# Skip term added as an accumulated row, step bias inside the projection, one product moved to GpSimd, and the split of the MLP input in a row of its own

## Chip, cores and metric

The kernel runs on 1 core of one Trainium2 chip. The metric is device time in microseconds (us) of one execution. The engines are named as in the profile: PE is TensorE, DVE is VectorE, ACT is ScalarE, POOL is GpSimd, SP is SyncE (here it only issues DMAs).

## What is computed

Eight samples of 384 channels by 32x32 tokens (L = 1024). Layer 0 is a hybrid of a bidirectional selective scan and a depthwise convolution, layer 1 is causal attention and an MLP:

```python
def mamba(x, ...):                       # once forward, once on the flipped tokens
    u, z = split(x @ in_proj_w.T)
    u = silu(causal_conv4(u) + conv1d_b)
    dt, B, C = split(u @ x_proj_w.T, [24, 40])
    delta = softplus(dt @ dt_proj_w.T + dt_proj_b)
    h = exp(delta * A) * h + (delta * u) * B      # 16 states per channel, over 1024 tokens
    y = sum_n h * C + u * D_param                 # the skip term is u * D_param
    return (y * silu(z)) @ out_proj_w.T
x = x + res_scale * ((fwd + bwd) * scale_mod + sigmoid(dwconv3x3(xn) + dw_b) * xn)
t = t + attention(layernorm(t))          # 6 heads of 64, causal, 1024 tokens
t = t + gelu(layernorm(t) @ kron(c_fc_1, c_fc_2).T) @ kron(c_proj_1, c_proj_2).T
```

## The kernel before

Each engine has its own hand-written program; semaphores tie them. Channels lie on partitions as 3 tiles (k = 0, 1, 2) of 128, tokens along the free dimension, so most operations are 128x1024 in float32. One iteration b does layer 0 of sample b and, beside it, layer 1 of sample b-1; iteration 0 has no layer 1, iteration 8 no layer 0. An iteration has two stages.

**Preparation.** ACT copies the projected u (`copy_u`), DVE does the 3x3 taps (`depthwise`) and the 4-tap filters of both directions (`causal`), `silu_u` on ACT makes uc[0] and uc[1]. `step_size` on PE projects dt into PSUM (`dt_bank`); softplus of forward is max(x,0) + log(1 + exp(-|x|)): `soft_abs`, `soft_exp` and `soft_log` on ACT, `relu` (L977) and `soft_sum` (L983) on DVE. `in_project(b, 1)` on PE projects z in six groups (t = 6 to 11) of which ACT takes the SiLU (L917); groups 8 and 9 use PSUM banks that held `dt_bank[2]`. DVE then scales the gate (L1162), POOL adds it to the residual (L1237), DVE writes the skip term of both directions into y (`skip`, L1044 and L1047) and multiplies delta by u (`times_u`, L993).

**96 rows.** Row r is one state n of one direction d for one channel tile k. ACT makes the decay exp(delta * A) in PSUM (`decay`, L716), POOL multiplies du by the row of B (`input_row`, L1213) into one of five buffers hb, DVE scans (`scan_row`, L1055) and multiplies by the row of C (`output_row`, L1064), and POOL issues a DMA that adds the result to y (`sum_row`, L1224), LAG = 2 rows later. Decay r needs row r-2 finished on DVE; input r needs the DMA of row r-5 landed. Backward softplus sits in the first rows as items `step_bc`, `step_in`, `step_log`, `step_sum`. ACT also stores the backward relu over xres, for which the residual must first have been copied to DRAM.

Layer 1 of sample b-1 is a list of items, ITEMS, each with a weight. `slots()` spreads the list over the 96 rows in proportion to the running weight; each engine executes, in row r, its part of the items of SLOTS[r], some "early" (ahead of the row's own scan on DVE, or of decay r+1 on ACT), some after it. `scores n` and `values n` (n = 0 to 27) are the attention's groups; CROWDED are groups n for which `values n-1` and `scores n` share a row, where the scaling of the context comes late instead of early. PE has no work of its own in the rows and runs the items in list order.

Of the kernel before, what the change touches and what calls it, by code (L numbers as in the profile page):

```python
# [16 lines left out]
ALU = mybir.AluOpType  # L17
ACT = mybir.ActivationFunctionType
# [6 lines left out]
NS = 16  # L25
# [14 lines left out]
YIN = 16 * 2 * NS  # L40
# [10 lines left out]
for _h in range(0, NH, 2):  # L51
# [20 lines left out]
    + [("ln_mean", 1, 0.8), ("ln_var", 1, 0.9), ("ln_scale", 1, 0.9), ("mlp_in", 0, 1.395)]  # L72
# [20 lines left out]
STEP = ("step_bc", "step_in", "step_log", "step_sum")  # L93
# [9 lines left out]
def hybrid_block(nc, x, chan, scal, k128, k32, w_in, w_x, w_dt, w_out, wq, wk, wv, wo, fc1, fc2, pr1, pr2, kept, bc_rows, out):  # L103
    with ExitStack() as ctx:
# [20 lines left out]
        dt_w = [mixed[32:32 + RANK, 0:C], mixed[96:96 + RANK, 0:C]]  # L125
# [17 lines left out]
        dtr = [narrow[32:32 + RANK, :], narrow[96:96 + RANK, :]]  # L143
# [139 lines left out]
        def _(sp):  # L283
# [70 lines left out]
            def iteration(b, layer0, layer1, more):  # L354
                if layer0:
# [49 lines left out]
        def _(pe):  # L405
# [18 lines left out]
            def in_project(b, part):  # L424
# [27 lines left out]
            def step_size(b, d, k):  # L452
# [49 lines left out]
            def item(kind, n, b):  # L502
# [174 lines left out]
        def _(act):  # L677
# [62 lines left out]

            def copy_u(b):
# [28 lines left out]
            def item(kind, n, b, early):  # L770
# [3 lines left out]
                elif kind == "step_in" and not early:  # L774
# [4 lines left out]
                    act.activation(delta[1][:, n, :], dt_bank[KT + n][:, :], ACT.Relu,  # L779
                                   bias=vec[:, n, V_DTB:V_DTB + 1]).then_inc(relu_done, 1)  # L780
# [104 lines left out]
            def iteration(b, layer0, layer1, more):  # L885
                if layer0:
# [56 lines left out]
        def _(dve):  # L943
# [93 lines left out]
            def skip(b, d):  # L1037

                for k in range(KT):
                    dve.wait_ge(uc_ready, at(6, b, 3 * d + k + 1))  # L1040
                    dcol = vec[:, k, V_D:V_D + 1]
                    if d == 0:
                        dve.wait_ge(op_ready, at(6, b, 0))
                        dve.tensor_scalar(y[:, k, :], uc[0][:, k, :], dcol, None, ALU.mult).then_inc(yd_ready, 1)  # L1044
                    else:
                        dve.wait_ge(yd_ready, at(6, b, k + 1))
                        dve.scalar_tensor_tensor(out=y[:, k, :], in0=uc[1][:, k, :], scalar=dcol,  # L1047
                                                 in1=y[:, k, :], op0=ALU.mult, op1=ALU.add).then_inc(yd_ready, 1)

            def scan_row(b, r, n, k, d):  # L1050
# [4 lines left out]
                dve.tensor_tensor_scan(flow(d, buf), flow(d, buf), flow(d, hb[r % NHB][:, :]), 0.0,  # L1055
                                       ALU.mult, ALU.add).then_inc(scan_done, 1)

            def output_row(b, r, n, k, d):
# [5 lines left out]
                dve.tensor_tensor(hb[r % NHB][:, :], pBC[r % 2][:, :], c_row[g % 2][:, :], ALU.mult)\  # L1064
                   .then_inc(m2_done, 1)

            def item(kind, n, b, early):
                a = b - 1
                if kind == "step_sum" and not early:
                    soft_sum(b, 1, n)  # L1070
                    times_u(b, 1, n)
# [41 lines left out]
                elif kind == "mlp_in" and not early:  # L1113
# [30 lines left out]
            def iteration(b, layer0, layer1, more):  # L1144
                if layer0:
# [8 lines left out]
                    for k in range(KT):  # L1154
                        relu(b, k)
# [8 lines left out]
                    skip(b, 0)  # L1164
                    skip(b, 1)
# [149 lines left out]
```

## Time and profile before

| | |
|---|---|
| median of 3 runs | 4690.36 us (4688.07 to 4693.26) |
| profiled execution, time and span | 4690.52 us, span 4688.3 us |
| DVE busy | 4013.4 us, 86% of the span |
| PE / ACT / POOL busy | 69% / 52% / 61% |
| mean granted TensorE clock | 0.798 of full |
| one of the 6 middle iterations (first scan to first scan) | 549.6 us: 448.2 in its rows, 101.4 in preparation |
| rows of the first iteration | 349.5 us |
| after the last row of iteration 7 | 339.6 us |

The scan of row 0 starts at 144.0 us in iteration 0, at 610.35 in iteration 1, at 1158.65 in iteration 2, and every 549.6 us from there. Iteration 2 is used below for the preparation and the first rows, iteration 1 for the late rows. A row of the timeline is: start in us, duration in us, engine and line, operation, tiles, shapes, how many were merged, and in brackets how long the engine had been idle and which instruction ended that.

### The profile page before, as it was taken

Reading aid. Unit: us, or ns where it says so; the run is one execution under the profiler, and the core shown is the slowest. Engines: PE = TensorE matmul, PEld = TensorE weight load, DVE = VectorE, ACT = ScalarE, POOL = GpSimd, SP = SyncE. Lnnn points to the kernel's source line nnn. Section 1 sums busy time; section 2 is a strip of 40 time slices with the busy share of each in tenths; the row PEclk is TensorE's granted clock in tenths of the full one; section 3 lists DMA queues with packets and bytes.
Section 4 is the critical chain, followed back from the end, with each engine's and each line's share of the span. In section 5 each row is a group of like instructions: output and inputs, shape, how many; then the busy total and the mean of one; then the engine's idle time right before and its main releaser. Section 6 shows DMA issues by size and latency. Waiting matters only on the chain.

```text
span 4688.3 us, 38816 instructions
## 1 busy us (share of the span) xinstructions
PE 3251.8 (69%) x10858; PEld 1667.3 (36%) x10858; DVE 4013.4 (86%) x2961; ACT 2447.6 (52%) x3430; POOL 2847.9 (61%) x1671
## 2 busy tenths in 40 slices
PE   4100677767777768777677777877687776777797
PEld 1000235512354224532255223542245322552372
DVE  5999899989898999989999898988989899998221
ACT  3433446555464555655466544656556554665262
POOL 2798467764676647765577646766477655776100
PEclk8555778877888878878788778888788877888898
DMA  2799469982788639885599828886388855988100
GB/s 85 181 248 246 103 144 206 216 210 77 186 197 216 163 101 207 201 216 131 133 207 207 211 80 188 199 217 167 98 200 200 216 147 123 206 201 186 51 6 14
DMA packets 223126, 772.34 MB, mean 165 GB/s; under 512 B 24666, under 2 KB 40330, under 8 KB 222890
## 3 DMA queue, kind: packets, MB, share of 16 engines
q0 software_dynamic: 110592, 402.70, 44.2%
q1 hardware_dynamic: 112298, 366.90, 24.4%
q8 instruction: 98, 1.61, 0.1%
q14 instruction: 138, 1.13, 0.1%
HBM read 339.60 MB, written 27.26 MB: 78 GB/s over the span
## 4 chain that ended last, share of the span: by engine, by line
DVE 33%; PE 23%; issue 22%; POOL 8%; ACT 8%; DMA 5%; DVEq 1%; SPq 0%; ACTq 0%; POOLq 0%
DVE pBC L1055 16%; POOL hb L1213 7%; PE pW L482 5%; DMA y<-hb 5%; PE pW L421 4%; PE pW L449 4%; DVE stat L1095 3%; PE pW L561 2%; DVE hb L1064 2%; DVE du_f L1008 2%; ACT pBC L716 1%; PE pW L586 1%; ACT area L865 1%; ACT L867 1%; DVE du_f L1162 1%
## 5 line engine op out<-in xcount | busy, mean ns | idle before, releaser
L1055 DVE TENSOR_TENSOR_SCAN pBC<-pBC,hb 128x1024 f32<-128x1024 f32 x768 | 1756.6, 2287 | 90.0 <-ACT pBC L716 53.9
L1224 POOL DMA_DIRECT2D y<-hb x768 | 722.8, 941 | 912.9 <-DVE hb L1064 844.6
L1213 POOL TENSOR_TENSOR hb<-du_f,b_row 128x1024 f32<-128x1024 f32 x384 | 1039.8, 2720 | 61.2 <-DVE du_f L993 48.6
L1213 POOL TENSOR_TENSOR hb<-uc_b,b_row 128x1024 f32<-128x1024 f32 x384 | 1000.1, 2605 | 48.6 <-DMA y<-hb 34.4
L1064 DVE TENSOR_TENSOR hb<-pBC,c_row 128x1024 f32<-128x1024 f32 x768 | 940.6, 1225 | 46.7 <-DVE pBC L1055 3.2
L716 ACT ACTIVATE pBC<-xres,vec 128x1024 f32<-128x1024 f32 x384 | 427.1, 1117 | 337.2 <-DVE hb L1064 336.3
L561 PE MATMUL pW<-area,pt 128*128 128x64 f32 x3456 | 446.4, 284 | 157.9 <-ACT pt L831 157.9
L716 ACT ACTIVATE pBC<-delta,vec 128x1024 f32<-128x1024 f32 x384 | 427.5, 1116 | 198.8 <-DVE hb L1064 198.7
L449 PE MATMUL pW<-area,consts 128*128 128x512 f32 x288 | 162.3, 723 | 487.0 <-ACT area L876 356.3
L561 PEld LDWEIGHTS pW<-area,pt 128*128 128x128 f32 x3456 | 417.5, 198 | 215.6 <-ACT pt L831 207.3
L1095 DVE TENSOR_REDUCE stat<-pW 128x1 f32<-128x640 f32 (+7 forms) x361 | 257.5, 750 | 166.5 <-PE pW L485 166.4
L482 PE MATMUL pW<-area,w_ko 128*128 128x512 f32 (+3 forms) x540 | 308.1, 708 | 123.8 <-ACT prob L841 85.0
L841 ACT ACTIVATE prob<-pW,stat 128x640 f32<-128x640 f32 (+7 forms) x361 | 265.3, 742 | 244.1 <-DVE stat L1095 244.1
L1232 POOL TENSOR_TENSOR du_f<-du_f,hb 128x1024 f32<-128x1024 f32 x64 | 193.4, 3022 | 254.0 <-ACT hb L730 248.5
L441 PE MATMUL pW<-area,xn_area 128*128 128x512 f32 x576 | 290.9, 665 | 62.5 <-DVE area L1138 55.4
L482 PE MATMUL pW<-area,v_w 128*128 128x512 f32 (+3 forms) x542 | 254.7, 600 | 45.3 <-ACT prob L841 45.0
L449 PEld LDWEIGHTS pW<-area,consts 128*128 128x128 f32 x288 | 64.4, 235 | 584.9 <-issue 462.4
L831 ACT COPY pt<-pW 128x512 f32<-128x512 f32 x378 | 209.1, 590 | 117.9 <-PE pW L498 113.9
L498 PE MATMUL pW<-consts,prob 128*128 128x128 f32 x1512 | 245.7, 311 | 29.3 <-ACT xn_area L757 16.5
L498 PEld LDWEIGHTS pW<-consts,prob 128*128 128x128 f32 x1512 | 199.0, 164 | 122.4 <-issue 119.3
L1008 DVE SCALAR_TENSOR_TENSOR du_f<-area,vec,du_f 128x1024 f32<-128x1024 f32 x128 | 227.6, 1846 | 0.0
L757 ACT ACTIVATE xn_area<-pW,stat 128x64 f32<-128x64 f32 x384 | 102.2, 310 | 220.4 <-DVE stat L1106 177.3
(158 smaller groups left out, 4969.1 us busy)
## 6 DMA issues: line engine op xcount, KB each, us to landing
y<-hb POOLq DMA_DIRECT2D x768, 512.0 KB, 7.0
b_row<-bc_rows SPq DMA_DIRECT2D x256, 512.0 KB, 5.8
c_row<-bc_rows SPq DMA_DIRECT2D x256, 512.0 KB, 5.0
area<-in_x SPq DMA_DIRECT2D x8, 1536.0 KB, 15.2
xres<-in_x SPq DMA_DIRECT2D x8, 1536.0 KB, 6.3
kept_residual<-xres SPq DMA_DIRECT2D x8, 1536.0 KB, 5.6
xres<-kept_residual SPq DMA_DIRECT2D x8, 1536.0 KB, 11.9
out_x<-xa SPq DMA_DIRECT2D x8, 1536.0 KB, 7.1
```

Source lines behind the costliest of these rows:

```text
L441: mm = pe.matmul(pW[:, t % 4, :], ip_w[:, k, 128 * m:128 * m + 128], xnp[:, k, 1 + 16 * c:17 + 16 * c, 1:1 + WW], start=(k == 0), stop=(k ...
L449: mm = pe.matmul(bank, ones_c, src[:, k, toks], start=(k == 0), stop=(k == KT - 1))
L482: pe.matmul(bank[:, lo:hi], q, kT[:, h // 2, lo - c0:hi - c0], start=True, stop=hi != end)
L498: mm = pe.transpose(prob_bank(b, half)[:, 128 * j:128 * j + 128], prob[:, half * HALF + 128 * j:half * HALF + 128 * j + 128], ident)
L561: mm = pe.matmul(pW[:, 3, DH * t:DH * t + DH], pt[:, c0 + 128 * j:c0 + 128 * j + 128], vtok[:, j, DH * h:DH * h + DH], start=(j == 0), sto ...
L716: act.activation(pBC[r % 2][:, :], delta[d][:, k, :], ACT.Exp, scale=vec[:, k, V_A + n:V_A + n + 1]).then_inc(da_ready, 1)
L1008: dve.scalar_tensor_tensor(out=acc, in0=win, scalar=w, in1=acc, op0=ALU.mult, op1=ALU.add).then_inc(dw_step, 1)
L1055: dve.tensor_tensor_scan(flow(d, buf), flow(d, buf), flow(d, hb[r % NHB][:, :]), 0.0, ALU.mult, ALU.add).then_inc(scan_done, 1)
L1064: dve.tensor_tensor(hb[r % NHB][:, :], pBC[r % 2][:, :], c_row[g % 2][:, :], ALU.mult)\
L1095: mx = dve.tensor_reduce(stat[:, 0, st:st + 1], scores_bank(b, n)[:, c0:c0 + 128 * (i + 1)], AX, ALU.max, negate=True)
L1213: pool.tensor_tensor(hb[r % NHB][:, :], du[d][:, k, :], b_row[g % 2][:, :], ALU.mult)\
L1224: pool.dma_start(y[:, k, :], hb[r % NHB][:, :], accum_op=ALU.add).then_inc(y_in[k], 16)
```

## The change

- `skip` leaves DVE. ACT computes u * D_param: forward into y ahead of decay 0, backward into hb[0..2] between decay 0 and the items of row 0. POOL adds the backward part to y with three more DMAs (`sum_skip`), issued ahead of the input of row 2. Rows use the buffers from hb[3] on (`slot`), so input r waits from row 2 on, at first for these DMAs.
- `relu` leaves DVE. The bias enters the projection as a 25th row, and `soft_sum` of the forward direction does max(x, 0) + log part in one operation, out of PSUM. With it, z groups 8 and 9 on PE wait for the third such sum.
- `times_u` of the backward direction is done by POOL, in rows 6, 9 and 12 (`step_du`).
- The DVE part of `mlp_in` becomes an item `mlp_split` of weight 0.7 behind it. The weights' sum grows from 103.16 to 103.86, by which items move by up to one row from row 17 on.

```diff
+for _k in range(KT):
+    SLOTS[6 + 3 * _k].append(("step_du", _k))
@@ ITEMS
-    + [("ln_mean", 1, 0.8), ("ln_var", 1, 0.9), ("ln_scale", 1, 0.9), ("mlp_in", 0, 1.395)]
+    + [("ln_mean", 1, 0.8), ("ln_var", 1, 0.9), ("ln_scale", 1, 0.9), ("mlp_in", 0, 1.395), ("mlp_split", 0, 0.7)]
@@ PE, in_project
                     elif t >= 8:
-                        pe.wait_ge(relu_done, at(6, b, 3))
-                        pe.wait_ge(sp_abs, at(6, b, 3))
+                        pe.wait_ge(delta_ready, at(6, b, 3))
@@ ACT
+            def skip(b, d):
+                for k in range(KT):
+                    act.wait_ge(uc_ready, at(6, b, 3 * d + k + 1))
+                    act.wait_ge(op_ready if d == 0 else delta_ready, at(6, b, 0 if d == 0 else k + 1))
+                    act.activation(y[:, k, :] if d == 0 else hb[k][:, :], uc[d][:, k, :], ACT.Identity,
+                                   scale=vec[:, k, V_D:V_D + 1]).then_inc(yd_ready, 1)
...
                     silu_u(b, 1)
                     act.preload_act_table_set(LOG_EXP)
+                    skip(b, 0)
                     decay(b, 0)
+                    skip(b, 1)
@@ DVE, soft_sum
                 if d == 0:
+                    dve.scalar_tensor_tensor(out=delta[0][:, k, :], in0=dt_bank[k][:, :], scalar=0.0,
+                                             in1=soft[0][k][:, :], op0=ALU.max, op1=ALU.add).then_inc(delta_ready, 1)
@@ DVE, iteration
-                    for k in range(KT):
-                        relu(b, k)
                     causal(b, 12, 24)
...
-                    skip(b, 0)
-                    skip(b, 1)
                     for k in range(KT):
-                        times_u(b, 0, k)
+                        times_u(b, k)
@@ POOL
+                elif kind == "step_du":
+                    pool.wait_ge(delta_ready, at(6, b, 4 + n))
+                    pool.wait_ge(yd_ready, at(6, b, 6))
+                    pool.tensor_tensor(du[1][:, n, :], delta[1][:, n, :], uc[1][:, n, :], ALU.mult).then_inc(du_ready, 1)
...
-                if r >= NHB:
-                    pool.wait_ge(y_in[(r - NHB) % KT], at(YIN, b, 16 * ((r - NHB) // KT + 1)))
+                if r >= NHB - KT:
+                    pool.wait_ge(y_in[(r + KT - NHB) % KT], at(YIN, b, 16 * ((r + KT - NHB) // KT + 1)))
...
+                        if r == NHB - KT:
+                            for skip_k in range(KT):
+                                sum_skip(b, skip_k)
```

On PE, the z groups 8 and 9 stand in the preparation of an iteration (the loop's body; area is the normalised input, xn_area the weights). Before:

```order
67 L441 MATMUL pW<-area,xn_area 128x512 [waits xd_evac]
68 L441 MATMUL pW<-area,xn_area 128x512 x2
69 L441 MATMUL pW<-area,xn_area 128x512 [waits sp_abs,relu_done]
70 L441 MATMUL pW<-area,xn_area 128x512 x2
71 L441 MATMUL pW<-area,xn_area 128x512 [waits sp_abs,relu_done]
72 L441 MATMUL pW<-area,xn_area 128x512 x2
```

and after the change:

```order
67 L447 MATMUL pW<-area,xn_area 128x512 [waits xd_evac]
68 L447 MATMUL pW<-area,xn_area 128x512 x2
69 L447 MATMUL pW<-area,xn_area 128x512 [waits delta_ready]
70 L447 MATMUL pW<-area,xn_area 128x512 x2
71 L447 MATMUL pW<-area,xn_area 128x512 [waits delta_ready]
72 L447 MATMUL pW<-area,xn_area 128x512 x2
```

Nothing moved on PE, but what groups 8 and 9 wait for did: DVE's relu stood ahead of its backward filters, the sum stands behind them.

On ACT, from the backward SiLU (L738, L746 after the change) to the first backward softplus item, before:

```order
123 L738 ACTIVATE uc_b<-uc_b,vec 128x1024 [waits cv_step]
124 L920 ACT_TABLE_LOAD
125 L713 ISA
126 L716 ACTIVATE pBC<-delta,vec 128x1024 [waits delta_ready,m2_done]
127 L688 REGISTER_ALU
128 L689 COPY narrow<-pW 24x1024 [waits xd_ready]
129 L690 COPY pt<-pW 32x1024
130 L716 ACTIVATE pBC<-delta,vec 128x1024 [waits delta_ready,m2_done]
```

and after the change:

```order
125 L746 ACTIVATE uc_b<-uc_b,vec 128x1024 [waits cv_step]
126 L935 ACT_TABLE_LOAD
127 L754 ACTIVATE y<-area,vec 128x1024 [waits op_ready,uc_ready] x3
128 L721 ISA
129 L724 ACTIVATE pBC<-delta,vec 128x1024 [waits delta_ready,m2_done]
130 L752 REGISTER_ALU
131 L754 ACTIVATE hb<-uc_b,vec 128x1024 [waits delta_ready,uc_ready]
132 L752 REGISTER_ALU
133 L754 ACTIVATE hb<-uc_b,vec 128x1024 [waits delta_ready,uc_ready]
134 L752 REGISTER_ALU
135 L754 ACTIVATE hb<-uc_b,vec 128x1024 [waits delta_ready,uc_ready]
```

Three operations stand ahead of decay 0 (pBC), three more between it and the copies that feed the backward step size.

On DVE, late in the rows (a scan is printed here as SCALAR_TENSOR_TENSOR pBC<-pBC,hb), from the last layer-norm scaling to the split of the MLP input, before:

```order
714 L1064 TENSOR_TENSOR hb<-pBC,c_row 128x1024 [waits scan_done,c_in1]
715 L1086 TENSOR_TENSOR area<-area,pW 128x3x512 [waits ln_rs] x2
716 L1114 ISA
717 L1115 TENSOR_TENSOR prob<-pW,pt 128x1024 [waits xr_step]
718 L1116 REGISTER_ALU
719 L1117 CAST pt<-prob 128x1024 [waits xr_step]
```

and after the change:

```order
698 L1084 TENSOR_TENSOR area<-area,pW 128x3x512 [waits ln_rs] x2
699 L1051 REGISTER_ALU
700 L1054 SCALAR_TENSOR_TENSOR pBC<-pBC,hb 128x1024 [waits m1_done,da_ready]
701 L1063 TENSOR_TENSOR hb<-pBC,c_row 128x1024 [waits scan_done,c_in1]
702 L1051 REGISTER_ALU
703 L1054 SCALAR_TENSOR_TENSOR pBC<-pBC,hb 128x1024 [waits m1_done,da_ready]
704 L1063 TENSOR_TENSOR hb<-pBC,c_row 128x1024 [waits scan_done]
705 L1112 ISA
706 L1113 TENSOR_TENSOR prob<-pW,pt 128x1024 [waits xr_step]
```

Two whole rows (scan and product) now stand between the scaling and the split. A little ahead of this, `ln_mean 1` moved from a row of its own (73) into row 72, right behind the last `wo` item; `wo 0` moved from row 69 to 68.

## Rows read from the trace of the kernel before

**Rows 1.** The page, part 1: busy time, share of the span, instructions.

```profile
PE 3251.8 (69%) x10858; PEld 1667.3 (36%) x10858; DVE 4013.4 (86%) x2961; ACT 2447.6 (52%) x3430; POOL 2847.9 (61%) x1671
```

**Rows 2.** Timeline of DVE, iteration 2, preparation and first rows.

```profile
1117.69 2.46 DVE L977 TENSOR_SCALAR delta<-pBC,vec 128x1024 f32<-128x1024 f32 x2
...
1121.27 2.06 DVE L1031 TENSOR_SCALAR uc_b<-area,vec 128x1024 f32<-128x1024 f32 x3
...
1134.02 3.48 DVE L983 TENSOR_TENSOR delta<-delta,hb 128x1024 f32<-128x1024 f32 x3
...
1143.10 6.24 DVE L1044 TENSOR_SCALAR y<-area,vec 128x1024 f32<-128x1024 f32 x3
...
1152.85 3.48 DVE L993 TENSOR_TENSOR du_f<-delta,area 128x1024 f32<-128x1024 f32 x3
1158.65 2.30 DVE L1055 TENSOR_TENSOR_SCAN pBC<-pBC,hb 128x1024 f32<-128x1024 f32 x1 [2.31 <-POOL hb L1213]
...
1162.20 2.29 DVE L1055 TENSOR_TENSOR_SCAN pBC<-pBC,hb 128x1024 f32<-128x1024 f32 x1
...
1187.76 2.29 DVE L1055 TENSOR_TENSOR_SCAN pBC<-pBC,hb 128x1024 f32<-128x1024 f32 x1
```

**Rows 3.** Timeline of ACT, the same stretch.

```profile
1132.54 3.21 ACT L738 ACTIVATE uc_b<-uc_b,vec 128x1024 f32<-128x1024 f32 x3
1135.77 1.28 ACT L920 ACT_TABLE_LOAD   x1
...
1143.92 1.00 ACT L690 COPY pt<-pW 32x1024 f32<-32x1024 f32 x1
...
1147.70 1.11 ACT L699 ACTIVATE area<-pW,vec 128x1024 f32<-128x1024 f32 x1 [1.77 <-PE pW L462]
...
1166.45 2.94 ACT L708 ACTIVATE area<-area 128x1024 f32<-128x1024 f32 x3
```

**Rows 4.** Timeline of PE, z projection (two passes a matmul).

```profile
1112.80 8.39 PE L441 MATMUL pW<-area,xn_area 128*128 128x512 f32 x12
1121.40 10.61 PE L441 MATMUL pW<-area,xn_area 128*128 128x512 f32 x24 [0.21 <-DVE delta L977]
```

**Rows 5.** Busy time by stretch: engines, then PEclk, DMA share, GB/s.

```profile
1112.90:1121.30 8.40, 8.29 (x12) 3.18 (x12) 8.40 (x8) 8.36 (x9) 0.20 (x1) 0.65 0.40 148
```

**Rows 6.** Timeline of POOL, iteration 2: gate sum, first inputs, a row's DMA.

```profile
1138.78 9.36 POOL L1237 TENSOR_TENSOR xres<-xres,du_f 128x1024 f32<-128x1024 f32 x3 [25.68 <-DVE du_f L1162]
...
1154.21 8.94 POOL L1213 TENSOR_TENSOR hb<-du_f,b_row 128x1024 f32<-128x1024 f32 x3 [6.08 <-DVE du_f L993]
...
1191.61 0.88 POOL L1224 DMA_DIRECT2D y<-hb  x1 [10.58 <-DVE hb L1064]
```

**Rows 7.** DVE groups by line and shape: count, busy us, mean ns, idle before.

```profile
L993 DVE TENSOR_TENSOR uc_b<-xres,uc_b 128x1024 f32<-128x1024 f32 x24 | 63.6, 2652 | 0.8
```

**Rows 8.** Line L1055, all scans: shortest, median, longest ns, first and last start.

```profile
L1055 DVE TENSOR_TENSOR_SCAN pBC<-pBC,hb x768: 2275/2289/2299, 144.0 to 4345.2; 128x1024 f32<-128x1024 f32 x192
```

**Rows 9.** The page, part 6, DMAs: count, size, us to landing.

```profile
y<-hb POOLq DMA_DIRECT2D x768, 512.0 KB, 7.0
```

**Rows 10.** Timeline of DVE, iteration 1, second layer norm and MLP input.

```profile
945.27 1.76 DVE L1078 TENSOR_TENSOR area<-xa,pW 128x1536 f32<-128x1536 f32 x1 [1.17 <-PE pW L449]
...
969.05 1.23 DVE L1115 TENSOR_TENSOR prob<-pW,pt 128x1024 f32<-128x1024 f32 x1 [9.13 <-ACT pt L857]
```

**Rows 11.** Timeline of DVE, iteration 1, attention: first and last of six waits.

```profile
739.92 1.29 DVE L1095 TENSOR_REDUCE stat<-pW 128x1 f32<-128x512 f32 x2 [0.19 <-PE pW L485]
...
894.16 1.29 DVE L1095 TENSOR_REDUCE stat<-pW 128x1 f32<-128x256 f32 x2 [1.67 <-PE pW L485]
```

**Rows 12.** Timelines of DVE and ACT, iteration 0; the last row is scan 4.

```profile
103.03 2.48 DVE L977 TENSOR_SCALAR delta<-pBC,vec 128x1024 f32<-128x1024 f32 x2 [8.33 <-ACT hb L699]
...
107.73 2.95 ACT L708 ACTIVATE hb<-hb 128x1024 f32<-128x1024 f32 x3
...
169.93 2.29 DVE L1055 TENSOR_TENSOR_SCAN pBC<-pBC,hb 128x1024 f32<-128x1024 f32 x1
```

More of the change, by code:

```diff
@@ L39 @@
 NHB = 5
-YIN = 16 * 2 * NS
+YIN = 16 * (2 * NS + 1)
 LAG = 2
@@ L124, in hybrid_block @@
         mixed = sb("mixed", [128, C])
[L125 removed]
+        dt_w = [mixed[32:33 + RANK, 0:C], mixed[96:97 + RANK, 0:C]]
         kout_w = mixed[64:64 + KI, 0:C]
@@ L142, in hybrid_block @@
         narrow = sb("narrow", [128, L])
-        dtr = [narrow[32:32 + RANK, :], narrow[96:96 + RANK, :]]
+        dtr = [narrow[32:33 + RANK, :], narrow[96:97 + RANK, :]]
         rr = narrow[64:64 + KI, :]
@@ L273, in rows, with slot @@
             return [(r, r // DROWS, r % DROWS // KT, r % KT) for r in range(ROWS)]
+        def slot(r):
+            return (r + KT) % NHB
         def flow(d, ap):
@@ L368, in iteration @@
                         sp.wait_ge(du_ready, at(6, b, 3))
+                        sp.wait_ge(yd_ready, at(6, b, 3))
                         load_next(b + 1)
@@ L458, in step_size @@
                 if g >= 4:
-                    pe.wait_ge(relu_done, at(6, b, g - 1))
-                    pe.wait_ge(sp_abs, at(6, b, g - 1))
+                    if g == 4:
+                        pe.wait_ge(delta_ready, at(6, b, 3))
+                    else:
+                        pe.wait_ge(relu_done, at(3, b, 1))
+                        pe.wait_ge(sp_abs, at(6, b, 4))
                 for c in range(2):
@@ L698, in soft_abs @@
                 act.wait_ge(dt_ready, at(6, b, 3 * d + k + 1))
-                act.activation(soft[d][k][:, :], dt_bank[KT * d + k][:, :], ACT.Abs,
-                               bias=vec[:, k, V_DTB:V_DTB + 1]).then_inc(sp_abs, 1)
+                act.activation(soft[d][k][:, :], dt_bank[KT * d + k][:, :], ACT.Abs).then_inc(sp_abs, 1)
             def soft_exp(b, d, k):
@@ L778, in item @@
                     act.wait_ge(kept_out, at(16, b, 16))
-                    act.activation(delta[1][:, n, :], dt_bank[KT + n][:, :], ACT.Relu,
-                                   bias=vec[:, n, V_DTB:V_DTB + 1]).then_inc(relu_done, 1)
+                    act.activation(delta[1][:, n, :], dt_bank[KT + n][:, :], ACT.Relu).then_inc(relu_done, 1)
                 elif kind == "step_log" and not early:
@@ L1035, in causal @@
                                                  op0=ALU.mult, op1=ALU.add).then_inc(cv_step, 1)
-            def skip(b, d):
-                for k in range(KT):
[L1040 to L1048, printed above, removed]
             def scan_row(b, r, n, k, d):
@@ L1112, in item @@
                                              in1=xa[:, m, toks], op0=ALU.add, op1=ALU.add).then_inc(wo_add, 1)
-                elif kind == "mlp_in" and not early:
+                elif kind == "mlp_split" and not early:
                     dve.wait_ge(xr_step, at(5, a, 1))
@@ L1153, in iteration @@
                     depthwise(b, 8, 18)
-                    for k in range(KT):
-                        relu(b, k)
                     causal(b, 12, 24)
@@ L1219, in sum_row, with sum_skip @@
                 pool.wait_ge(m2_done, at(ROWS, b, r + 1))
-                if r < KT:
-                    pool.wait_ge(yd_ready, at(6, b, 6))
-                else:
-                    pool.wait_ge(y_in[k], at(YIN, b, 16 * (r // KT)))
-                pool.dma_start(y[:, k, :], hb[r % NHB][:, :], accum_op=ALU.add).then_inc(y_in[k], 16)
+                pool.wait_ge(y_in[k], at(YIN, b, 16 * (r // KT + 1)))
+                pool.dma_start(y[:, k, :], hb[slot(r)][:, :], accum_op=ALU.add).then_inc(y_in[k], 16)
+            def sum_skip(b, k):
+                pool.wait_ge(yd_ready, at(6, b, 4 + k))
+                pool.dma_start(y[:, k, :], hb[k][:, :], accum_op=ALU.add).then_inc(y_in[k], 16)
             def iteration(b, layer0, layer1, more):
@@ L1297 @@
         "w_x": np.concatenate([xp[RANK:], xp[:RANK]], 0).T,
-        "w_dt": i0["dt_proj_w"].T,
+        "w_dt": np.concatenate([i0["dt_proj_w"].T, i0["dt_proj_b"][None]], 0),
         "w_out": i0["out_proj_w"].T,
```

38 lines of the change are left out of this document (16 added, 22 removed).

## Prediction

> **What bounds it now.** I read the page first, then the timeline of DVE, then the same stretches of ACT, PE and POOL. The page [rows 1] shows DVE busy 86% of the span and everybody else at 69% or less. The timeline of DVE shows why: a row of scan and product takes 3.5 us of DVE (scan 1 starts 3.55 after scan 0), 96 rows follow each other almost without idle time, and in the preparation (depthwise, filters, sums, gate, skip, product with u) DVE waits for nobody but POOL, 2.3 us ahead of scan 0 [rows 2]. So a microsecond taken from DVE is a microsecond of the kernel, as long as no other engine's work has to be done by then. That condition is the whole question here, because the change puts work on ACT and makes PE wait.
>
> **What leaves DVE, per iteration.** relu: from 1117.69 to 1121.27, 3.6 us. skip: from 1143.10 to 1152.85, 9.75 us. [rows 2] The backward product with u: 3 x 2.65 = 7.95 us [rows 7]. Together 21.3 us, over eight iterations 170 us. If all of it counted, the kernel would be at 4520.
>
> **The preparation, on the clock of iteration 2.** DVE ends the depthwise taps at 1117.7 as before. The filters last 12.75 us (1121.27 to 1134.02) and now start 3.6 earlier: 1130.4. The three new sums read PSUM and SBUF; no such row exists, the nearest are the old relu (3.6 for three) and the old sums (3.48), so 3.5: 1133.9. [rows 2]
>
> PE: z groups 8 to 11 were 10.61 us from 1121.4 [rows 4]. They now wait for the third sum, 1133.9, so 12.5 us later. PE has then been idle for some 13 us. How it restarts is in the trace: the first z groups took 8.39 us for 12 passes, with a granted clock of 0.65, where 5.3 would be the time at the full level [rows 4, 5]. So a restart costs between nothing and 3.1 us; I take 2.3, as the longer idle time speaks for most of it. PE ends at 1146.9.
>
> ACT can't pass these groups: its order is fixed. Last SiLU of z 1147.5, three backward SiLUs 3.2, table 1.3: 1152.0. Three skip products: no row has them, but three 128x1024 activations in a row took 3.2: 1155.2. Decay 0, 1.1 as each of those: 1156.3. Three more skip products: 1159.5. Two copies, 2.0: 1161.5. Decay 1: 1162.6. The first backward |x| comes 2.8 after the copies (1144.9 to 1147.7): 1164.3. Two triples (abs, exp, relu; 3.1 each): 1170.5. Decay 2: 1171.6. Third triple: 1174.7. Three logs, 2.9: 1177.6. Decay 3: 1178.7. [rows 3]
>
> POOL and DVE by themselves would be earlier. The gate sum on POOL moves with DVE's gate, 3.5 earlier, and ends at 1144.6 instead of 1148.1 [rows 6]; the product with u can start there (it was at 1152.85), and scan 0 came 5.8 after its start [rows 2]: 1150.4. The decay is ready at 1156.3, so **ACT sets scan 0**, only 2.3 us ahead of the old 1158.65. Then scan 1 waits for decay 1 (1162.6), scan 2 for decay 2 (1171.6), scan 3 for decay 3 (1178.7). From there DVE: row 3.5, two sums 2.5 (1.2 each as the forward ones), layer-norm mean 3.3 (two of 1.76, overlapping a little) [rows 10], scan 4 at 1188.0. Before it was at 1187.76 [rows 2]. **So the 21 us that leave DVE give nothing: +0.2 us per iteration**; DVE stands idle instead, in rows 0 to 3, for the decays.
>
> What this hides: the skip's DMAs. They are issued from about 1158 on and land 7.0 later [rows 9], so input 2 is done by 1168, ahead of decay 2 at 1171.6. If the ACT chain were 6 us shorter, it would cost. The three products on POOL in rows 6, 9 and 12 are 2.65 each; POOL runs two rows ahead, and waits 10.58 us for DVE at the first [rows 6]. At the other two its lead of about one row (3.5) takes the 2.65. I cost them at nothing; with the cover gone, up to 8 us per iteration.
>
> A page of the Trainium skill speaks against this step. Perfetto Trace Analysis, section Optimizing Scalar/DVE Operations, warns that DVE and GpSimd share an SBUF read port and that moving operations between those two "might not help". By that rule, the page's own words, the 8 us would only change place. What the trace shows is that the DVE product took 2.65 us beside POOL's work instead of the 1.16 of the forward one, but the scans keep 2275 to 2299 ns throughout [rows 2, 7, 8]: in the rows DVE isn't blocked by POOL. The sum goes by this.
>
> **Iteration 0** differs: there DVE waited 8.33 us at the relu for ACT [rows 12]. Now the filters fill that wait and the third sum follows the logs, which end at 110.7: 112.0. With the same chain as above (44.7 us from third sum to decay 3, 54.1 to scan 4) scan 4 is at 166.1; it was at 169.9 [rows 12]. Gain 3.8 us.
>
> **The late rows** (iterations 1 to 7). DVE waited 9.13 us for the MLP input to come out of PE and ACT [rows 10]. Two rows now stand there, 7.0 us: that much is gained. Against it, the second layer-norm mean stands right behind the last wo item. Its averages start only then, and the row that covered them but for 1.17 us [rows 10] is gone: 3.5 us lost. wo 0, a row earlier, waits a little more: 0.3. Net 3.2 gained at the split. Behind it ACT's Gelu and table loads share the pacing with DVE, and one row less stands ahead of the first Gelu; I take 0.9 as given back. 2.3 per iteration; bounds 0 and 3.5.
>
> **Attention.** Of its pairs of groups in adjacent rows, those whose scores come late make DVE wait, between 0.19 and 1.67 us, six times in iteration 1 [rows 11]. The new slots have eight such pairs, as before, but other groups: five instead of six begin with a two-block group. At unchanged odds that is -0.5 us per iteration. Each wait is either near 0.2 or near 1.7, so the bounds are wide: from -6 to +6.3.
>
> **Sum.** Iteration 0: -3.8. Seven iterations: +0.2 - 2.3 - 0.5 = -2.6 each, -18.2. The tail, 339.6 us, keeps its order and its time. From the profiled execution's 4690.5: 4668.5; the median of the runs shown is 0.2 us below that execution, so **4668**.
>
> **Rivals.**
> - *The chain through the z groups is longer.* If the four z groups run at the low level throughout, they take 21.2 us instead of 12.9: +8.3 on ACT's chain and on every scan 4, eight times, 66 us: 4734. Point of decision: 2.8 us more per iteration than I have and the change is slower than before. For it: in rows 0 to 3 nothing covers ACT any more. Against: the trace's restart was over after 8.4 us. 12%.
> - *The chain does not bind*, DVE and POOL set the start: scan 0 at 1150.4 and rows 2 and 3 shorter by 7.95, 16.4 per iteration and 2.8 in seven, 151 us: 4540. It needs ACT 16 us faster than the rows give. 5%.
> - *Attention waits fall badly* (+6.3 in each of seven, 4715), 8%, *or well* (-6, 4630), 10%.
> - *The gain at the split is given back* to ACT's Gelu chain: 2.3 x 7 = 16, 4684. For it: rows behind the split wait for decays already. 12%.
> - *The product on POOL blocks DVE or falls into a full POOL*: 8 per iteration, 64 us, 4732. This is the skill's warning above turned into a time. 3%.
>
> **How the numbers follow.** My forecast has 50%, its own range 4645 to 4690. Cases outside 4622 to 4715 hold 12 + 5 + 3 = 20%, hence the range. 0.2% is about what a measurement of this kernel can tell from no change: 4681 to 4700. Faster: most of the 50 (42), attention well 10, chain not binding 5, part of the split case 4, so 61%. Same: 7 of the 50, 8 of the split case and a little of attention, 16%. Slower: 23%.
>
> **What the profile after would show.** z groups of L447 starting near 1134 less the shift of the earlier iterations; DVE idle before the first four scans, released by ACT's decays, 15 to 20 us in all; scan 4 as far from the end of the last row as before; the wait at the split about 2 us instead of 9.13, the wait at the second mean about 4.6 instead of 1.17; POOL's new products with no scan waiting behind them. I am wrong if scans 0 to 3 wait for POOL or the DMA instead, if z ends more than 15 us after the third sum, or if DVE's row times change.

## The result: 4751 us, 1.3% slower than before

| | before | changed |
|---|---|---|
| median (lowest to highest, 4 runs each) | 4691.4 us (4688.1 to 4693.3) | 4751.4 us (4746.4 to 4753.5) |
| ratio to before, 95% interval | | 1.0128 (1.0116 to 1.0140) |
| span of the profiled execution | 4688.3 us | 4748.2 us |

The page of the changed kernel, part 1, against [rows 1]:

```profile
PE 3277.8 (69%) x10858; PEld 1671.2 (35%) x10858; DVE 3901.6 (82%) x2865; ACT 2492.2 (52%) x3478; POOL 2935.0 (62%) x1719
```

DVE is 112 us less busy and the kernel 60 us longer: its idle time grew by 172 us. The starts of the scans say where the 60 are. I cut the trace at scans 0, 4, 66, 77 and 95 and added up iterations 1 to 7. The first column runs from the end of the last product of one iteration to scan 0 of the next:

| us | last product to scan 0 | 0 to 4 | 4 to 66 | 66 to 77 | 77 to 95 | iteration 0 | all |
|---|---|---|---|---|---|---|---|
| my sum | -16 | +17.5 | -3.5 | -22.4 | +6.3 | -3.8 | -22 |
| measured | -21.7 | +53.8 | -5.1 | +5.2 | +16.7 | +11.5 | +60 |

Three places miss: rows 0 to 4 (+36 against the sum), the late rows (+38) and iteration 0 (+15).

First the preparation and rows 0 to 4 of iteration 2, in the timelines of the changed kernel; DVE, to [rows 2]:

```profile
1151.34 2.34 DVE L994 SCALAR_TENSOR_TENSOR delta<-pBC,hb 128x1024 f32<-128x1024 f32 x2
1153.60 1.21 DVE L994 SCALAR_TENSOR_TENSOR delta<-pW,hb 128x1024 f32<-128x1024 f32 x1
...
1165.13 5.66 DVE L1005 TENSOR_TENSOR du_f<-delta,area 128x1024 f32<-128x1024 f32 x3 [4.64 <-POOL xres L1238]
1176.28 2.30 DVE L1054 TENSOR_TENSOR_SCAN pBC<-pBC,hb 128x1024 f32<-128x1024 f32 x1 [5.50 <-ACT pBC L724]
...
1182.49 2.30 DVE L1054 TENSOR_TENSOR_SCAN pBC<-pBC,hb 128x1024 f32<-128x1024 f32 x1 [2.58 <-ACT pBC L724]
...
1192.59 2.30 DVE L1054 TENSOR_TENSOR_SCAN pBC<-pBC,hb 128x1024 f32<-128x1024 f32 x1 [6.54 <-ACT pBC L724]
...
1199.38 2.30 DVE L1054 TENSOR_TENSOR_SCAN pBC<-pBC,hb 128x1024 f32<-128x1024 f32 x1 [1.68 <-ACT pBC L724]
...
1202.92 7.01 DVE L998 TENSOR_TENSOR xres<-xres,area 128x1024 f32<-128x1024 f32 x2
1209.85 3.40 DVE L1076 TENSOR_TENSOR xn_area<-xa,pW 128x1536 f32<-128x1536 f32 x2
1213.18 2.28 DVE L1054 TENSOR_TENSOR_SCAN pBC<-pBC,hb 128x1024 f32<-128x1024 f32 x1
```

PE, to [rows 4], and ACT, to [rows 3]:

```profile
1154.87 12.10 PE L447 MATMUL pW<-area,xn_area 128*128 128x512 f32 x24 [13.88 <-DVE delta L994]
```

```profile
1167.00 0.60 ACT L932 ACTIVATE zs<-pW 128x512 f32<-128x512 f32 x1 [1.99 <-PE pW L447]
1167.49 3.22 ACT L746 ACTIVATE uc_b<-uc_b,vec 128x1024 f32<-128x1024 f32 x3
1170.72 1.28 ACT L935 ACT_TABLE_LOAD   x1
1172.02 3.23 ACT L754 ACTIVATE y<-area,vec 128x1024 f32<-128x1024 f32 x3
1175.15 1.10 ACT L724 ACTIVATE pBC<-delta,vec 128x1024 f32<-128x1024 f32 x1
1176.19 3.21 ACT L754 ACTIVATE hb<-uc_b,vec 128x1024 f32<-128x1024 f32 x3
...
1198.24 2.15 ACT L724 ACTIVATE pBC<-delta,vec 128x1024 f32<-128x1024 f32 x2
```

ACT's chain is the one I built: z starts when the third sum (L994) ends and takes 12.1 us, then come SiLU, table load, skip products and decay 0. Each of scans 0 to 3 waits for a decay, 16.3 us in all. What doesn't fit stands behind scan 3: the last two backward sums (L998) take 7.01 us, not 2.5. POOL, to [rows 6], runs the new product (L1201) and an input (L1212) beside them:

```profile
1203.91 2.64 POOL L1201 TENSOR_TENSOR uc_b<-xres,uc_b 128x1024 f32<-128x1024 f32 x1
1206.30 2.54 POOL L1212 TENSOR_TENSOR hb<-du_f,b_row 128x1024 f32<-128x1024 f32 x1
```

Over the whole kernel, the groups of the changed kernel (first) and of before (second; those of [rows 7] have left DVE): count, busy us, mean ns:

```profile
L998 DVE TENSOR_TENSOR xres<-xres,area 128x1024 f32<-128x1024 f32 x24 | 65.9, 2771 | 2.6 <-ACT area L716 2.6
```

```profile
L983 DVE TENSOR_TENSOR xres<-xres,area 128x1024 f32<-128x1024 f32 x24 | 31.9, 1329 | 0.0
```

In iteration 0 POOL's four tap sums started beside DVE's ten tap steps (two SBUF inputs each) in the kernel before too, but DVE's backward filters came later, behind its wait at the relu. Now the filters follow the tap steps almost at once. DVE, POOL and ACT before (first), then POOL, ACT and DVE of the changed kernel:

```profile
82.66 12.04 DVE L1008 SCALAR_TENSOR_TENSOR du_f<-area,vec,du_f 128x1024 f32<-128x1024 f32 x10
...
85.04 19.32 POOL L1232 TENSOR_TENSOR du_f<-du_f,hb 128x1024 f32<-128x1024 f32 x4 [10.56 <-ACT hb L730]
...
96.92 1.15 ACT L730 ACTIVATE hb<-area,vec 128x1024 f32<-128x1024 f32 x1 [3.53 <-POOL du_f L1232]
```

```profile
83.85 32.07 POOL L1233 TENSOR_TENSOR du_f<-du_f,hb 128x1024 f32<-128x1024 f32 x4 [10.56 <-ACT hb L738]
...
108.49 1.15 ACT L738 ACTIVATE hb<-area,vec 128x1024 f32<-128x1024 f32 x1 [16.61 <-POOL du_f L1233]
...
81.48 12.03 DVE L1020 SCALAR_TENSOR_TENSOR du_f<-area,vec,du_f 128x1024 f32<-128x1024 f32 x10
...
95.42 10.84 DVE L1046 SCALAR_TENSOR_TENSOR uc_b<-area,vec,uc_b 128x1024 f32<-128x1024 f32 x9
120.10 2.36 DVE L994 SCALAR_TENSOR_TENSOR delta<-pBC,hb 128x1024 f32<-128x1024 f32 x2 [13.84 <-ACT hb L716]
```

DVE's filters keep their 1.2 us each, and POOL's sums take 32.1 us instead of 19.3. The whole difference lies in the first of the four, which takes 24.6 us instead of 11.9; the other three take 2.3 to 2.4 each in both kernels. The first ends 2.2 us after DVE's last step of this kind, before (94.7 and 96.9) and after (106.3 and 108.5). ACT waits 16.6 us for the tap, and the sum 13.8 us for ACT. In e1 below, where the forward sums stand ahead of the filters again, POOL's four are back at 19.3.

Late rows. Before, iteration 1, beside [rows 10]: DVE's only wait at the wo items, and PE at the averages:

```profile
926.79 0.75 DVE L1111 SCALAR_TENSOR_TENSOR xa<-pW,vec,xa 128x512 f32<-128x512 f32 x1 [1.03 <-PE pW L421]
...
940.69 7.12 PE L449 MATMUL pW<-xa,consts 128*128 128x512 f32 x12 [3.64 <-DVE xa L1111]
```

Changed, iteration 2: DVE at the first wo item, PE at the averages, DVE at the second mean (two operations) and the split:

```profile
1499.05 0.75 DVE L1109 SCALAR_TENSOR_TENSOR xa<-pW,vec,xa 128x512 f32<-128x512 f32 x1 [3.58 <-PE pW L428]
...
1517.13 8.38 PE L455 MATMUL pW<-xa,consts 128*128 128x512 f32 x12 [5.07 <-DVE xa L1109]
...
1522.66 1.75 DVE L1076 TENSOR_TENSOR area<-xa,pW 128x1536 f32<-128x1536 f32 x1 [5.58 <-PE pW L455]
1525.55 1.75 DVE L1076 TENSOR_TENSOR area<-xa,pW 128x1536 f32<-128x1536 f32 x1 [1.14 <-PE pW L455]
...
1547.08 1.22 DVE L1113 TENSOR_TENSOR prob<-pW,pt 128x1024 f32<-128x1024 f32 x1 [2.52 <-ACT pt L872]
```

The split waits 2.5 us instead of 9.1, near the 2 that I wrote. The mean waits 6.7, where I wrote 4.6, and wo 0 3.6.

### The profile page after: what moved, and what is told of

It is laid out like the page before. It is cut to its first block, busy times and chain, and to the rows that moved or that the text cites. A ratio compares the mean times of both kernels' runs of the same rounds, so it can differ in the third digit from the quotient of the medians.

```text
span 4748.2 us, 38811 instructions
## 1 busy us (share of the span) xinstructions
PE 3277.8 (69%) x10858; PEld 1671.2 (35%) x10858; DVE 3901.6 (82%) x2865; ACT 2492.2 (52%) x3478; POOL 2935.0 (62%) x1719
## 4 chain that ended last, share of the span: by engine, by line
DVE 28%; PE 27%; issue 20%; ACT 11%; POOL 8%; DMA 5%; DVEq 1%; SPq 0%; ACTq 0%; POOLq 0%
DVE pBC L1054 13%; PE pW L491 6%; POOL hb L1212 6%; DMA y<-hb 5%; PE pW L455 4%; DVE stat L1093 3%; PE pW L447 3%; PE pW L570 3%; PE pW L428 2%; ACT pBC L724 2%; DVE du_f L1020 1%; DVE hb L1063 1%; PE pW L595 1%; ACT area L880 1%; PE pW L471 1%
## 5 line engine op out<-in xcount | busy, mean ns | idle before, releaser
L1220 POOL DMA_DIRECT2D y<-hb x768 | 738.1, 961 | 934.3 <-DVE hb L1063 885.1
L1212 POOL TENSOR_TENSOR hb<-du_f,b_row 128x1024 f32<-128x1024 f32 x384 | 1044.8, 2735 | 42.7 <-DMA y<-hb 30.1
L1212 POOL TENSOR_TENSOR hb<-uc_b,b_row 128x1024 f32<-128x1024 f32 x384 | 1009.0, 2628 | 22.0 <-DMA y<-hb 21.9
L1063 DVE TENSOR_TENSOR hb<-pBC,c_row 128x1024 f32<-128x1024 f32 x768 | 940.2, 1224 | 44.7 <-DVE pBC L1054 0.5
L447 PE MATMUL pW<-area,xn_area 128*128 128x512 f32 x576 | 303.1, 689 | 168.0 <-DVE delta L994 113.1
L1233 POOL TENSOR_TENSOR du_f<-du_f,hb 128x1024 f32<-128x1024 f32 x64 | 206.5, 3226 | 249.6 <-ACT hb L738 244.1
L491 PE MATMUL pW<-area,w_ko 128*128 128x512 f32 (+3 forms) x540 | 281.6, 656 | 106.7 <-ACT prob L856 70.5
L491 PE MATMUL pW<-area,v_w 128*128 128x512 f32 (+3 forms) x542 | 264.9, 619 | 74.3 <-ACT prob L856 74.3
L447 PEld LDWEIGHTS pW<-area,xn_area 128*128 128x128 f32 x576 | 125.3, 223 | 351.2 <-issue 213.0
```

The source lines that it names most:

```text
L447: mm = pe.matmul(pW[:, t % 4, :], ip_w[:, k, 128 * m:128 * m + 128], xnp[:, k, 1 + 16 * c:17 + 16 * c, 1:1 + WW], start=(k == 0), stop=(k ...
L491: pe.matmul(bank[:, lo:hi], q, kT[:, h // 2, lo - c0:hi - c0], start=True, stop=hi != end)
L1063: dve.tensor_tensor(hb[slot(r)][:, :], pBC[r % 2][:, :], c_row[g % 2][:, :], ALU.mult)\
L1212: pool.tensor_tensor(hb[slot(r)][:, :], du[d][:, k, :], b_row[g % 2][:, :], ALU.mult)\
L1220: pool.dma_start(y[:, k, :], hb[slot(r)][:, :], accum_op=ALU.add).then_inc(y_in[k], 16)
```

## Experiments

Two theories about the 60 us stood first. **A, the z wait**: z groups 8 and 9 wait for a sum that stands behind the filters, and ACT, in fixed order, carries that to all decays. **B, DVE and POOL**: the work put on POOL is what costs. A third, **C**: the split's row costs more than it gives. The table has medians in us and ratios to before with their intervals; the stage columns are iteration 2 in one profiled execution ("gap" is the first column of the table above, the others go from scan to scan).

| | median | ratio | gap to scan 0 | 0 to 4 | 66 to 77 | 77 to 95 |
|---|---|---|---|---|---|---|
| before | 4691 | 1 | 101.4 | 29.1 | 65.5 | 77.6 |
| changed | 4751 | 1.0128 | 98.1 | 36.9 | 66.5 | 80.0 |
| sum_first | 4668 | 0.9953 (0.9936 to 0.9970) | 92.9 | 30.6 | 66.4 | 80.2 |
| du_a_row_later | 4745 | 1.0115 (1.0098 to 1.0132) | 98.1 | 34.6 | 66.5 | 80.3 |
| split_with_mlp_in | 4728 | 1.0079 (1.0063 to 1.0096) | 99.3 | 35.7 | 65.5 | 77.6 |
| before_with_split | 4713 | 1.0046 (1.0030 to 1.0063) | 101.3 | 29.1 | 66.4 | 80.2 |
| sum_first_old_rows | 4641 | 0.9888 (0.9870 to 0.9906) | 92.9 | 30.6 | 65.2 | 79.2 |
| before_z_wait | 4751 | 1.0125 (1.0107 to 1.0143) | 103.6 | 34.7 | 65.0 | 79.1 |
| changed_skip_on_dve | 4722 | 1.0063 (1.0045 to 1.0081) | 99.9 | 31.9 | 66.5 | 80.2 |
| sum_first_product_on_dve | 4670 | 0.9956 (0.9940 to 0.9971) | 92.9 | 32.0 | 66.5 | 80.3 |
| sums_from_psum | 4615 | 0.9831 (0.9813 to 0.9848) | 92.9 | 23.2 | 66.4 | 80.2 |
| best_product_row_later | 4617 | 0.9838 (0.9825 to 0.9852) | 92.9 | 28.3 | 65.0 | 79.1 |
| before_skip_on_act | 4667 | 0.9950 (0.9934 to 0.9965) | 96.1 | 32.0 | 65.0 | 79.1 |

**e1_sum_first.** The changed kernel, forward sums ahead of the backward filters:

```diff
                     depthwise(b, 8, 18)
-                    causal(b, 12, 24)
                     for k in range(KT):
                         soft_sum(b, 0, k)
+                    causal(b, 12, 24)
```

> The changed kernel, but the three forward sums (L994) stand on DVE ahead of the twelve backward filter steps instead of behind them. Theory A (the start of the rows is set by ACT's chain, which hangs on the z groups, which wait for the third sum): the sums wait about 2 us for ACT's logs, then z groups 8 to 11 start some 12 us earlier; ACT gets to decay 0 ahead of DVE and POOL, and from one of the iterations 1 to 7 about 5 to 9 us go: 4751 - 8 x 7 = about 4695 (4680 to 4710). Rival B (the wait of the z groups is harmless, the rows are held by work moved to GpSimd and by its DMAs): within 8 us of the changed kernel, 4743 to 4760.

83 us less than the changed kernel, more than A expected: 38 ahead of scan 0 and 44 in rows 0 to 4 of iterations 1 to 7, 9 in iteration 0, while other rows give back 7. No scan of rows 0 to 3 waits for a decay any more. The timeline of DVE shows what it waits for instead:

```profile
1143.08 5.64 DVE L1005 TENSOR_TENSOR du_f<-delta,area 128x1024 f32<-128x1024 f32 x3 [6.97 <-POOL xres L1238]
...
1158.08 2.30 DVE L1054 TENSOR_TENSOR_SCAN pBC<-pBC,hb 128x1024 f32<-128x1024 f32 x1 [2.36 <-POOL hb L1212]
...
1161.55 3.96 DVE L998 TENSOR_TENSOR xres<-xres,area 128x1024 f32<-128x1024 f32 x1
...
1168.97 7.01 DVE L998 TENSOR_TENSOR xres<-xres,area 128x1024 f32<-128x1024 f32 x2
```

POOL, the input of row 2:

```profile
1155.64 2.34 POOL L1212 TENSOR_TENSOR hb<-du_f,b_row 128x1024 f32<-128x1024 f32 x1 [2.12 <-DMA y<-hb]
```

The product with u waits for POOL's gate sum, scan 2 for POOL's input, and the input for the skip's DMA. The backward sums are as long as in the changed kernel or longer.

**e6_before_z_wait.** The kernel before, with nothing changed but what z groups 8 and 9 wait for:

```diff
                     elif t >= 8:
-                        pe.wait_ge(relu_done, at(6, b, 3))
-                        pe.wait_ge(sp_abs, at(6, b, 3))
+                        pe.wait_ge(delta_ready, at(6, b, 3))
```

> The kernel before with one edit: z groups 8 and 9 wait for the third forward sum, as in the change, instead of for the relu. Nothing is added to ACT and nothing leaves DVE. Theory A (z late by 16 us drags ACT's chain past DVE by itself): decay 2 some 8 us behind DVE's need, scan 3 and scan 4 about 8 us later in each of eight iterations: 4691 + 60 = 4750 (4730 to 4760). Rival B (ACT had the room, only z late together with six skip products on ACT costs): under 4700.

That wait alone costs 60 us, so A holds. 16 lie ahead of scan 0 and 38.5 in rows 0 to 4 of iterations 1 to 7, and 10 in iteration 0; other rows give back 3. PE and ACT in iteration 2 (the third sum of DVE ended at 1156.2):

```profile
1156.23 12.22 PE L440 MATMUL pW<-area,xn_area 128*128 128x512 f32 x24 [17.26 <-DVE delta L982]
1172.24 7.05 PE L642 MATMUL pW<-uc_b,xp_w 128*56 128x512 f32 x12 [3.80 <-ACT uc_b L737]
```

```profile
1168.98 3.21 ACT L737 ACTIVATE uc_b<-uc_b,vec 128x1024 f32<-128x1024 f32 x3
...
1179.33 1.00 ACT L688 COPY narrow<-pW 24x1024 f32<-24x1024 f32 x1 [4.71 <-PE pW L642]
```

A late z makes the backward SiLU late, its projection on PE later, and the copies and decays behind it.

**e3_split_with_mlp_in and e4_before_with_split.** The split's item shares a row with `mlp_in` again (weights 0.0 and 1.395, the old sum), and the kernel before gets the split's row and nothing else:

```diff
-    ... ("mlp_in", 0, 1.395), ("mlp_split", 0, 0.7)]
+    ... ("mlp_in", 0, 0.0), ("mlp_split", 0, 1.395)]
```

> The changed kernel, but the split shares the row and the weight of mlp_in again, so that all items but the products with u stand in their old rows. Theory A (the moved items cost: in rows 66 to 95 the changed kernel is 3.4 us per iteration slower than the kernel before): 7 x 3.4 less, 4728. Rival B (my forecast, the split's own row gains 2.3 us per iteration and the loss comes from what ACT and the clock do elsewhere): 16 us more, 4767.

> The kernel before with only the new item mlp_split of weight 0.7, which moves the slots as in the change. Theory A (the moved items cost 3 to 4 us in each of seven iterations by themselves): 4691 + 24 = 4715. Rival B (my forecast for this part alone, late rows -2.3 and attention -0.5 per iteration): 4671. If it is within 5 us of 4691, the late rows' loss in the changed kernel comes from its other parts.

The two agree: the split's row, with the shift of the items that it brings, costs 22 to 23 us, 3 per iteration. C holds, beside A.

**e5_sum_first_old_rows.** e1 and e3 together.

> Both repairs together: the forward sums ahead of the backward filters and the split in the row and weight of mlp_in, all else as in the changed kernel. If the two losses are separate, the gains add: 4668.5 - 23 = 4645 (4638 to 4652), 1% faster than the kernel before. If they overlap (the late rows are slower only because of what happened earlier in an iteration), between 4655 and 4668.

The two gains add up, and 5 us more come on top (27.6 instead of 23).

**e7_changed_skip_on_dve and e12_before_skip_on_act.** The skip moved by itself: in the changed kernel back to DVE (no skip DMAs), and in the kernel before to ACT, with its DMAs. Of e7 this is the part on ACT; DVE's skip and POOL's old buffer order come back with it:

```diff
                     act.preload_act_table_set(LOG_EXP)
-                    skip(b, 0)
                     decay(b, 0)
-                    skip(b, 1)
...
```

> The changed kernel with the skip term back on DVE and without its DMAs and the shifted buffers. Theory A (in rows 0 to 3 ACT's chain sets the pace, 6.4 us of it are the skip products; DVE has the room for the skip while it waits): 8 x 5 to 8 x 6.4 less than 4751, 4700 to 4711, though DVE does 9.8 us more work per iteration. Rival B (DVE's work sets the pace): 8 x 6 to 8 x 9.8 more, 4799 or above.

> The kernel before with the skip term alone moved: ACT computes it, GpSimd adds the backward part with three more DMAs, buffers shifted; relu, bias, products, z waits and items as before. Theory A (ACT had room for six more activations as long as z came early; DVE then waits only for the gate sum of GpSimd): scan 0 some 4.7 us earlier, 8 x 4.6 = 37 us less, 4654 (4645 to 4665). Rival B (the skip's DMAs or ACT hold rows 1 to 3, so the part costs by itself): 4691 or more.

The sign turns with what binds. Where z waits, 9.8 us more on DVE in each iteration make the kernel 29 us faster, since ACT's chain gets 6.4 us shorter. I expected 40 to 51: rows 0 to 4 give 34 in iterations 1 to 7, but DVE's skip now stands ahead of scan 0, and the gap takes 11 back. Where z doesn't wait, the move to ACT gains 24 us. That is less than the 37 I expected: the gap shrinks by 5.3, but scan 2 now waits 2.4 us for an input that waits for the skip's DMA, and in all 0 to 4 is 2.9 longer.

**e2_du_a_row_later.** POOL's products in rows 7, 10 and 13, a row behind the sums' rows.

```diff
 for _k in range(KT):
-    SLOTS[6 + 3 * _k].append(("step_du", _k))
+    SLOTS[7 + 3 * _k].append(("step_du", _k))
```

> The changed kernel, but the three backward products with u on GpSimd stand in rows 7, 10 and 13 instead of 6, 9 and 12. GpSimd runs ahead, so the product of row 6 runs while DVE does the second and third backward sum, which took 7.0 us for two. Theory A (an operation of DVE with two SBUF inputs and a GpSimd operation exclude each other): only the input of row 6 stands beside the sums then, the pair takes 4.7 us or less, 2.3 us less per iteration, 18 us: 4733. Rival B (the 7.0 us come from waiting for ACT or from the DMAs): no change, 4751. Rival C (GpSimd has no room in rows 7 to 13): slower than 4751.

Rows 0 to 4 get 2.3 us shorter, as expected; the kernel gets 6 us faster, not 18. Iteration 0 came out 3 longer, and rows 4 to 66 gave back 9 in iterations 1 to 7. In iteration 2 these are waits of DVE: before scans 6.1 us for 4.7, before the attention's reductions 10.5 for 8.8. Why they grow I have not found.

**e8_sum_first_product_on_dve and e9_sums_from_psum.** Both start from e1. e8 has the three products back on DVE, behind each sum. e9 leaves the products on POOL and lets the backward sum read PSUM instead of xres, so that one input lies in SBUF and not two; it reads half a projection twice and so leaves out a part of the backward step size. It waits for all three relus and the last projection. Its edit, shortened and without the waits:

```diff
-                    dve.tensor_tensor(delta[1][:, k, :], delta[1][:, k, :], soft[1][k][:, :], ALU.add)
+                    dve.scalar_tensor_tensor(out=delta[1][:, k, :]...,
+                                             in0=pW[:, 3:4, :].broadcast_to([128, 2, HALF]), scalar=0.0,
+                                             in1=soft[1][k][:, :]..., op0=ALU.max, op1=ALU.add)
```

> The kernel of e1_sum_first, but the three backward products with u are back on DVE, each right behind its sum, and none is on GpSimd. Theory A (the move to GpSimd gave almost nothing, because GpSimd's product holds up the sum beside it: sums and products took 12.2 us of DVE before, the sums alone 11.0 in e1_sum_first): 1.2 us more per iteration, 10 us, 4678 (4670 to 4685). Rival B (the move is worth what left DVE, 7.95 us per iteration): 4732.

> The kernel of e1_sum_first, but the three backward sums take max(x,0) from one PSUM bank (read twice) instead of from xres, so they have one SBUF input instead of two. It leaves out part of the computation: the backward step size of all three channel tiles takes half a row of the third one's projection. Number and size of DVE's operations are the same. Theory A (the sums took 11.0 us for three because an operation with two SBUF inputs and GpSimd's products exclude each other): three sums 3.6 us, up to 7.3 us less per iteration, 4610 to 4625. Rival B (they wait for ACT's logs or for DMAs, or the operation is slow by itself): within 5 us of 4668.

The groups of the sum in e1, of sum and product in e8, and of the sum in e9:

```profile
L998 DVE TENSOR_TENSOR xres<-xres,area 128x1024 f32<-128x1024 f32 x24 | 85.4, 3586 | 0.0
```

```profile
L998 DVE TENSOR_TENSOR xres<-xres,area 128x1024 f32<-128x1024 f32 x24 | 51.0, 2124 | 0.0
L1072 DVE TENSOR_TENSOR uc_b<-xres,uc_b 128x1024 f32<-128x1024 f32 x24 | 47.4, 1975 | 1.4
```

```profile
L999 DVE SCALAR_TENSOR_TENSOR xres<-pW,area 128x1024 f32<-128x1024 f32 x24 | 28.5, 1215 | 0.0
```

With the product on POOL the sum takes 3586 ns on average, as one of a pair on DVE 2124, and with one input in PSUM 1215. Taking 47.4 us of product from DVE gives 13 (98.4 to 85.4) on DVE and 2 in the kernel (I expected 10), within what the measurement can tell. Taking the second SBUF input away gives 53 on the kernel. So B falls as a cause of the 60 us, since with the products back on DVE the kernel is no faster; but the conflict of two SBUF inputs is why their move gave nothing.

**e10_best_product_row_later.** e5 with the products a row later.

> The kernel of e5_sum_first_old_rows with the products on GpSimd in rows 7, 10 and 13. Theory A (2.3 us less per iteration beside the sums, as in e2_du_a_row_later, of which some returns in rows 4 to 20): 4641 - 8 = 4633 (4622 to 4639). Rival B (all of it returns later): 4641 within 4.

It is the fastest version that computes everything, 1.6% ahead of before, and 24 us ahead of e5, 16 more than I expected. DVE's sums in iteration 2:

```profile
1155.19 3.94 DVE L998 TENSOR_TENSOR xres<-xres,area 128x1024 f32<-128x1024 f32 x1
...
1162.59 4.73 DVE L998 TENSOR_TENSOR xres<-xres,area 128x1024 f32<-128x1024 f32 x2
```

e1 and e5 have 7.01 for the two, since there POOL's product and an input stand beside the last one and here only an input. Over the kernel the sums fall from 87.7 us in e5 to 59.3, more than iteration 2 shows, and rows 0 to 4 of iterations 1 to 7 get 23.7 us shorter, as much as the medians gain.

## Why the prediction was wrong

I forecast 4668; it is 4751, beyond the upper bound, on the other side of before. Three steps failed. None of my three signs of being wrong came up (scans 0 to 3 waited for decays, z ended 12.2 us after the third sum, DVE's row times stayed): none of them looked at the sums, at iteration 0 or at the late rows.

**"The three products on POOL ... I cost them at nothing."** I had the objection in hand and took it off the table with the wrong row. The Trainium skill, Perfetto Trace Analysis, Optimizing Scalar/DVE Operations, warned of the shared port. I looked whether the scans kept their time, and they do (2.28 to 2.30 us in the timeline after). But a scan reads PSUM and one SBUF input. The sums and the product with u read two. A row for those was in front of me: the backward product took 2652 ns in [rows 7], and a forward one 1.16 us from start to start. I read that as what DVE would save; it was mostly the time it stood blocked, and it went over to the sums: 63.6 us of product left DVE and the sums grew from 31.9 to 65.9. Unblocked, each takes 1.21 us. Before, the 24 sums and 24 products took 95.5 us where 58 would do; after, the 24 sums took 65.9 where 29 would do. In these sums and products DVE lost 37 us to the conflict both times. By this, rows 0 to 4 came out 4.5 us longer than the forecast per iteration; it is most of the 36. The Trainium skill, SBUF — State Buffer, Who interferes with whom, has the finer rule: a DVE instruction with two SBUF inputs contends with a GpSimd instruction that reads SBUF, and one with at most one, outside the two-port modes, doesn't. e9 agrees with it: 3586 ns against 1215. The rival that I gave 3% was this one, at half its price.

**Iteration 0, "Gain 3.8 us".** It lost 11.5. Pulling the filters forward into DVE's wait set them beside POOL's tap sums, with the same two-input conflict, this time against POOL: +12.8 us there, handed to ACT's taps and from ACT to the sums. The third sum ends at 123.6 where I had 112.0, and scan 4 starts at 178.6 where I had 166.1. In e1, without filters beside POOL, the third sum ends at 112.1. I took the wait as free room and did not ask who runs in it.

**The late rows, "2.3 per iteration".** Measured it is a loss of 3.1 (21.9 us in seven iterations; 22.2 in e4, on the kernel before). The gain was sized right (wait at the split 9.1 to 2.4 us, here and below as means over iterations 1 to 7). The losses were not: the second mean went from 2.0 to 6.6 (I had +3.5), the first wo items and the row ahead of them from 1.7 to 4.4 (I had +0.3, though wo 0 loses a row of cover just as the mean does), and the rows behind gave back 2.4, not 0.9. The averages ran at a lower granted clock as well: 8.38 us for 12 at 0.64, where 12 took 7.12 at 0.76 before.

**What held.** ACT's chain: 44.7 us from the third sum to decay 3 in my sum, 44.6 in the trace. The z restart: 1.5 over the old 10.61, inside my bounds 0 to 3.1, at a granted clock of 0.87, where it was 1.00 before. "So the 21 us that leave DVE give nothing": all four scans wait for decays. Attention: waits fell by 0.5 per iteration, as I had it. But this chain was also where the prize lay. I laid the z wait down as neutral because ACT ended up where DVE had been; it had eaten everything that the rest of the change gained. e6 prices it at 60 us by itself, and e1 gives back 83. That the whole change comes to the same 60 is a coincidence: the skip on ACT alone gives 24, and the split alone costs 22.

**Open.** In iteration 0, e1 takes DVE's filters away from POOL's sums and starts z earlier, both at once; the two were not taken apart there, and that iteration accounts for 9 of the 83 us (505.0 to 495.9). In iterations 1 to 7 the backward filters take 1.27 to 1.28 us each in both kernels and POOL's tap sums 23 to 24 us, so what e1 gains there is not that conflict. Not explained is the part of e2 that came back elsewhere explained. The projection's bias row was not tried alone.

## What to carry to other kernels

Before moving an operation from DVE to POOL, look at the SBUF inputs of what DVE does at that moment: an elementwise operation with two of them pays (2.1 to 3.6 us instead of 1.2 here), a scan or a sum with only one of its inputs in SBUF didn't, and a DVE duration well over its unblocked twin (2.65 against 1.21) is blocked time that the move won't remove. When an edit changes only what an instruction waits for, follow the in-order engine behind it to its end, and ask whether two blocks can change places on the producer: here the same three sums, one block earlier, were worth 83 us. A row of cover that goes to one wait is taken from all the waits that it stood in front of.

## What was not expected of the hardware

- The conflict goes both ways, and the engine that comes second can be held through several instructions of the other. One POOL sum took 24.6 us beside DVE's ten tap steps and nine filters (none of them longer for it), 11.9 beside the tap steps alone and 2.3 with neither. Beside POOL's products and inputs, DVE's sum took 3.6 us on average instead of 1.2.
- How long a DVE operation is held depends on what POOL has beside it: with POOL's product a row later, two sums took 4.73 us instead of 7.01, and the kernel 4617 instead of 4641.
